# Three stages of a written-out plan on one Trainium2 core: the logits product one step earlier, two output norms three and two steps earlier, one G product one step later

## The reference, cut to what matters

```python
x = L0_attn_x                                            # (8, 1024, 256)
x = _layernorm(x + _L0_attn_ref(x, ...), axis=-1)        # x1 below
x = _layernorm(x + _L0_ffn_ref(x, expert_sel, keys, values), axis=-1)
# attention: q, k, v from x; squares of q and k, normalised; kv = k2^T v; (v + q2 kv) Wln + bln
sel    = sigmoid(einsum('bsd,ed->bse', x1, expert_sel))  # 16 gates a row: the "logits" are its argument
scores = relu(einsum('bsd,edh->bseh', x1, keys))         # "up"
out    = einsum('bseh,ehv,bse->bsv', scores, values, sel)# "gate", then "down"
```

## Time and profile before

| | us |
|---|---|
| median of 3 runs | 1011.67 (1010.37 to 1012.95) |
| the profiled execution, device time | 1008.1 |
| its span, first to last instruction | 1006.1 |
| PE busy | 982.1 (98%) |
| DVE busy | 805.2 (80%) |
| ACT busy | 526.9 (52%) |
| granted TensorE clock, mean | 0.995 |

### The profile page before, as it was taken

The page is one execution under the profiler, slowest core; times in us unless marked ns, Lnnn a source line. Parts: engine busy times, 40 slices in busy tenths (PEclk is TensorE's granted clock), DMA queues, the critical chain, the costliest instruction groups (busy, mean ns, idle before and its releaser), DMA issues.

```text
span 1006.1 us, 20851 instructions
## 1 busy us (share of the span) xinstructions
PE 982.1 (98%) x7700; PEld 939.0 (93%) x7700; DVE 805.2 (80%) x1874; ACT 526.9 (52%) x1150; POOL 55.1 (5%) x75
## 2 busy tenths in 40 slices
PE   7899999999999999999999999999999999999996
PEld 6799999999999999999999999999999999999996
DVE  5889877888879887788878888788887888878545
ACT  4566544566355753556536565366644656454323
POOL 0010100101010010100101001010100101010100
PEclk8999999999999999999999999999999999999999
DMA  6054133352344323442333522425133352333221
GB/s 187 22 177 139 61 110 114 112 155 75 106 134 137 98 86 116 141 141 75 100 118 126 160 77 93 145 83 193 56 113 108 109 166 68 111 102 110 90 95 63
DMA packets 75624, 112.45 MB, mean 112 GB/s; under 512 B 7170, under 2 KB 37634, under 8 KB 75524
## 3 DMA queue, kind: packets, MB, share of 16 engines
q1 hardware_dynamic: 75524, 111.13, 34.3%
HBM read 87.51 MB, written 23.46 MB: 110 GB/s over the span
## 4 chain that ended last, share of the span: by engine, by line
PE 72%; DVE 12%; DMA 6%; issue 5%; ACT 3%; SPq 2%; POOL 0%; DVEq 0%; ACTq 0%; POOLq 0%
PE up_bank L1370 25%; PE down_bank L1370 25%; PE ring_bank L1370 9%; PE qk_bank L1370 7%; PE g_bank L1370 3%; DMA sel_all<-sel_out 3%; DVE gated_l L1113 2%; DMA parked_x<-w_room 2%; DVE gated L1131 2%; SPq L457 2%; DVE x1T_l L978 1%; DVE qk L1131 1%; ACT L646 1%; ACT z L721 1%; DVE z_stats L1075 1%
## 5 line engine op out<-in xcount | busy, mean ns | idle before, releaser
L1370 PE MATMUL down_bank<-vals_h,gated_h 128*128 128x256 f32 x1024 | 285.6, 279 | 4.9 <-DVE gated_l L1113 4.6
L1370 PE MATMUL down_bank<-vals_l,gated_h 128*128 128x256 f32 x1024 | 283.2, 277 | 0.0
L1370 PE MATMUL down_bank<-vals_h,gated_l 128*128 128x256 f32 x1024 | 283.2, 277 | 0.0
L1370 PE MATMUL up_bank<-x1T_l,keys_h 128*128 128x256 f32 (+1 forms) x928 | 267.7, 288 | 0.0
L1370 PE MATMUL up_bank<-x1T_h,keys_l 128*128 128x256 f32 (+1 forms) x928 | 267.7, 288 | 0.0
L1370 PE MATMUL up_bank<-x1T_h,keys_h 128*128 128x256 f32 (+1 forms) x928 | 267.6, 288 | 0.0
L578 ACT ACTIVATE gated_h<-gated 128x512 fp32r<-128x512 f32 x176 | 111.1, 631 | 196.4 <-DVE gated L1131 196.4
L1370 PEld LDWEIGHTS down_bank<-vals_h,gated_h 128*128 128x128 f32 x1024 | 192.3, 188 | 11.9 <-DVE gated_l L1113 7.6
L1370 PEld LDWEIGHTS down_bank<-vals_l,gated_h 128*128 128x128 f32 x1024 | 192.4, 188 | 4.1
L1370 PEld LDWEIGHTS down_bank<-vals_h,gated_l 128*128 128x128 f32 x1024 | 192.3, 188 | 0.0
L1131 DVE SCALAR_TENSOR_TENSOR gated<-up_bank,sel_all 128x512 f32<-128x512 f32 x176 | 121.3, 689 | 76.3 <-PE up_bank L1370 54.9
(11 more groups left out here) (259 smaller groups left out, 1774.4 us busy)
## 6 DMA issues: line engine op xcount, KB each, us to landing
sel_all<-sel_out SPq DMA_DIRECT2D x192, 256.0 KB, 3.8
out<-z SPq DMA_DIRECT2D x32, 256.0 KB, 2.5
x_raw<-in_x SPq DMA_DIRECT2D x15, 512.0 KB, 5.7
xT_raw<-in_xT SPq DMA_DIRECT2D x14, 512.0 KB, 5.6
parked_q<-w_room SPq DMA_DIRECT2D x14, 512.0 KB, 2.6
q<-parked_q SPq DMA_DIRECT2D x56, 128.0 KB, 3.0
parked_x<-w_room SPq DMA_DIRECT2D x14, 512.0 KB, 3.4
w_room<-parked_x SPq DMA_DIRECT2D x56, 128.0 KB, 3.0
```

The lines of the kernel that those rows point to most:

```text
L1370: last = mm(dst, lhs, rhs, start=start and i == 0, stop=stop and i == n - 1, **kw)
```

## The change

Three entries of the table move. LG 0 goes from step 30 to step 29. ZN 0 goes from 29 to 26 and ZN 1 from 30 to 28. GG 0 goes from step 9 to step 10, in front of GG 1. No instruction is added or taken away.

```diff
-        9: [("GG", 0)], 10: [("XR", 1), ("QK", 2), ("GG", 1)], 11: [("QK", 3), ("QS", 0)],
+        9: [], 10: [("XR", 1), ("QK", 2), ("GG", 0), ("GG", 1)],
...
-        25: [("QR", 1), ("XS", 3)], 27: [("XR", 0)], 29: [("ZN", 0)], 30: [("LG", 0), ("ZN", 1)],
+        25: [("QR", 1), ("XS", 3)], 26: [("ZN", 0)], 27: [("XR", 0)], 28: [("ZN", 1)], 29: [("LG", 0)],
```

## The result

The changed kernel takes 1025.65 us (median of 4 runs, 1024.92 to 1028.35) against 1011.07 for the kernel before (4 runs): a ratio of 1.0147, 95% interval 1.0127 to 1.0167, so 14.6 us slower. The forecast was 1024.5. The profiled execution took 1025.27 us against 1008.1: 17.2 more. Of these, 2.6 come from where the two executions lie: the one of before was 3.0 us under its median, this one 0.4.

What follows compares the result with a forecast made beforehand. PE, busy 98% of the span, was taken to bound the kernel. Logits product 12.5 + spread row 2.8 - waits gone 2.4 = 12.9 us, on 1011.67 giving 1024.6; forecast 1024.5, range 1018.5 to 1032.

Steps and rivals of the forecast that it cites:

- likeliest case: Logits product waits for its input and spread rows cost 0 to 5 us: +9 to +16 us, chance 0.55.
- The product waits for its input at each of seven ends: Step 29: PE stands 1.7 to 2.4 us at the logits product; down(29) is later by 12.5 us over seven ends.
- Down(29) waits for the spread row of gate(30): The row, issued behind store and xT load, makes down(29) wait 0.47 us at six batch ends, 2.8 us in all.
- The waits of down(31) go: Sel is ready earlier relative to gate(0), so down(31) stops waiting at six batch ends: -2.4 us.
- G product, norms on DVE and ACT: First G product at step 10 only shifts time between steps 9 and 10; early norms' DVE and ACT work is covered: 0 us.
- what would make me wrong: Product finds its input ready, PE's wait there well below 1.5 us, down(26) waits, or granted clock falls after the stalls.
- a price of the logits product: Batch ends, product moved to step 29: its wait for input delays down(29), 12.5 us over seven ends.
- a price of the store: SP list at step 26: store of pair 0 waits for ACT's passes and delays gate(30)'s spread row, 2.8 us.
- The forecast of the norms alone: Norms at 26 and 28, logits at 30: down(29) waits for gate(30)'s row, +11 to +14 us, ratio 1.011 to 1.014.

Runs made afterwards that it cites:

- first experiment: Kernel before with the logits product alone at step 29, norms left at 29 and 30 and G at 9: 1027.38 us, ratio 1.0149.
- late stores: Changed kernel with SP issuing the stores of steps 26 and 28 behind the rows of sel: 1025.02 us, 1.0146; run again 1029.99 us, 1.0185.
- filler: Changed kernel with seven matmuls that nothing reads ahead of the logits product's wait: 1027.13 us, 1.0172; with the stores behind the rows of sel too, 1021.63 us, 1.0117.
- late stores and the added second wait: Changed kernel, stores behind the rows of sel, with PE taking down(29) only after gate(31): 1034.53 us, ratio 1.0206.

## Why the prediction was right

**Direction and size: right.** 12.9 us were forecast, 14.6 measured in the medians; the 1025.65 lies in the likeliest case's range. One of the two mechanisms alone (first experiment) would have given it. That the median came within 1.2 us of the forecast is in part luck: the profiled executions lie 17.2 us apart, and the terms below miss by +1.8, +1.15, +3.3 (a term that the sum did not have) and -2.6 us, and 0.85 more is no part of the change.

**The product waits for its input at each of seven ends: right, and its size.** Forecast 12.5 us for down(29). Measured from the account: the product starts 2.17 us after the start of the copies where 2.08 was taken, and takes 0.1 us longer behind a wait (its first matmul 0.47 in its row against 0.39); that is 1.4 us over seven ends, with 0.4 for the input, which was taken as unmoved. 12.5 + 1.4 + 0.4 = 14.3. The waits themselves were put at 1.7 to 2.4 us and came to 1.58 to 2.92: three just under, the sixth over.

**Down(29) waits for the spread row of gate(30): right in kind, its size at five ends.** Forecast 0.47 at six ends, 2.8; measured in starts 0.55, 0.78, 0.96, 1.00 and 0.66 at ends 2, 3, 4, 5 and 7, together 3.95 (the rows of waits say 3.0). The row landed 4.9 us after its issue where 4.45 was taken, at all seven ends after 4.0 to 5.3. End 7 was counted out for having no load of xT, and that step was wrong: with only the store ahead of it, its row took 5.3 us, the longest of all. At the other six ends the row landed 0.6 to 1.9 us after the load of xT. That agrees with the ring order in which, by the Trainium skill, "DMA: Bandwidth & Descriptors", section "Queues, rings and completion order", each DMA engine consumes descriptors; the order of landing that section leaves open. The estimate of 3.5 us by that page's fit in its section on the anatomy of a DMA was too low, and would have made this term nothing; the fit is given for DMAs that GpSimd issues, one by one, and these are three in a row that SP issues.

**The waits of down(31) go: right, too small.** Forecast -2.4, measured -4.3 behind the first six ends. The forecast took the idle time of the rows. A wait costs more than that: idle is counted from the modelled end of the last matmul, 0.28 us after its start where the next would start after 0.11, and the first matmul behind it has 0.39 us. Some 0.27 more for each of six waits is 1.6, so 4.0; the rest is small differences in step 1 and behind. The other 0.7 of the 5.0 that come back lie at the end of the kernel and were not in the sum.

**G product, norms on DVE and ACT: nothing, right**, shown by the runs with the G product alone and with the norms early and the stores late.

**What the sum did not have: the clock.** It stood only under what would make me wrong. At ends 1 and 6 down(29) starts 1.55 and 1.73 us later after the product than its work takes, without waiting: 3.3 us. Some 0.8 at each, what the other five ends wait on average, is the second wait's place taken. The terms as measured: 14.3 + 3.95 + 3.3 - 5.0 + 0.85 (start) = 17.4, the 17.3 of above but for rounding.

**What was wrong in the structure.** I added a price of the logits product and a price of the store. The runs with one of them alone cost 1.0149 and 1.0173, together 1.0147: each would do the whole harm, and what stands first hides the other. My 2.8 us were the part of the second by which it exceeds the first, which is why the sum came out; read as "what the norms cost", it was wrong by some 15 us. The forecast of the norms alone, made after the result, still missed the falls of the clock at three of its ends.

## What to carry to other kernels

When two edits each delay the same point, work out when each would reach it and take the later one; to learn what one of them costs, run it alone, and to gain anything, undo both. In a list that is kept in order, a store that waits for computed data goes behind the loads that have nothing to wait for: here that was the difference between +1.7% and -0.2% for the same early norms. And price a standstill of PE at more than its idle row: add the start-up of the first matmul, and look for the granted clock behind it. At full clock and without an idle row, compare the pitch of the matmuls too: the page's busy share does not tell a slow one.

## What the hardware showed that was not expected

**The clock falls after some standstills of 1.8 to 3.4 us, and not after others.** In the changed kernel it fell at waits of 2.17 and 2.92 us and not at 2.11 and 2.34, and in its repetition at other ends, once at a wait of 1.82. Over the traces of all kernels here there are 22 falls at the batch ends. All seven waits of 2.8 us and more had one, 15 of the 25 between 1.82 and 2.7 us, and none of the shorter ones. In the changed kernel the clock stayed at 0.50 for 3.4 us each time (in the late stores again once for 6.8) and cost about 1.6 us. With the filler in front, the part of the waits in which PE was idle came to at most 1.7 us, and the clock did not fall. What decides between two equal waits stays open.

**A longer pitch at full clock.** Behind the product's wait, PE can go on for some 50 us with matmuls of 128x256 that start every 0.118 us where 0.113 is normal. The same matmuls in the same stretch (190 to 226 us) of the kernel with late stores (its second run) and of the changed kernel (last columns: count, busy us, mean ns, idle):

```profile
L1373 PE MATMUL down_bank<-vals_h,gated_l 128*128 128x256 f32 x36 | 10.1, 281 | 0.0
```

```profile
L1370 PE MATMUL down_bank<-vals_h,gated_l 128*128 128x256 f32 x36 | 9.9, 276 | 0.0
```

and the clock in the former:

```profile
180.00:200.00 20.00, 20.00 (x166) 19.74 (x165) 16.97 (x43) 9.29 (x16) 1.00 (x2) 1.00 0.20 68
```

The clock is 1.00 and nothing waits, yet 5 ns are lost at each of these matmuls.

In each trace 6775 matmuls of 128x256 follow another one. So many of them start 116 to 120 ns behind it:

| kernel | starts after 116 to 120 ns |
|---|---|
| before | 637 |
| changed; its repetition | 573; 812 |
| three other runs in which down(29) waits at seven ends | 661 to 792 |
| product alone at 29 | 1682 |
| late stores; again | 1611; 2511 |
| product behind down(27) and late stores | 2006 |
| filler and late stores | 1471 |
| early norms with late stores, product at 30 | 999 |
| late stores and the added second wait | 1075 |

They are many where no wait at down(29) or down(31) follows the product's. At 4.5 ns each, what goes beyond the 637 is an estimated 8 us in the longest case, 5 with the product alone, 4 in the first run with late stores and 6 with both edits of product and stores. That is of the size by which these runs lie above their expectations, and would be a reason why taking the second wait away gained nothing; the falls of the clock are another, and the two were not told apart.

But a standstill is not what ends the long ones: of 16 stretches of over 50 us, 14 run on to about step 12 of the next batch and two, behind the last end, further, and all end without any idle time of PE. What sets this rhythm, and what ends it, is not shown.
